# The degree count's matmuls with their operands swapped: the 49-wide one-hot stationary, the 128-wide one moving

## The reference, cut to what matters

```python
deg = jnp.maximum(jax.ops.segment_sum(jnp.ones(dst.shape, jnp.float32), dst, num_segments=6250), 1.0)
...
deg_isqrt = 1.0 / jnp.sqrt(node_deg)
f0 = f0 * deg_isqrt                      # features before the edges gather them
...
s_mid = s_mid * deg_isqrt                # sums of messages after the edges
```

## Time and profile before

| | |
|---|---|
| median of 3 timed runs | 4400.84 us (4399.68 to 4402.47) |
| profiled execution: span | 4400.9 us |
| PE busy / PEld busy in the span | 4086.7 us (93%) / 3374.9 us (77%) |
| DVE, ACT, POOL busy | 2987.8, 2610.6, 2599.1 us |
| node loop, 91.2 to 440.6 us: PE busy | 349.4 of 349.4 us |

### The profile page before, as it was taken

The page is one execution under the profiler, slowest core; times in us unless marked ns, Lnnn a source line. Parts: engine busy times, 40 slices in busy tenths (PEclk is TensorE's granted clock), DMA queues, the critical chain, the costliest instruction groups (busy, mean ns, idle before and its releaser), DMA issues. The chain is left out here.

```text
span 4400.9 us, 84837 instructions
## 1 busy us (share of the span) xinstructions
PE 4086.7 (93%) x19450; PEld 3374.9 (77%) x19450; DVE 2987.8 (68%) x5419; ACT 2610.6 (59%) x8831; POOL 2599.1 (59%) x2378
## 2 busy tenths in 40 slices
PE   4999599999999999999999999999985888888887
PEld 3888488888888888888888888888985777777776
DVE  5666699999999999999999999997666000000000
ACT  1444587888788878887888787776232222222222
POOL 3444577777777777777777777775113233333332
PEclk8999799999999999999999999999967999999999
DMA  3333333443444333433443444433223455555554
GB/s 117 103 101 98 116 103 103 104 104 103 104 104 104 104 104 104 103 103 104 104 104 103 103 103 104 104 103 85 79 80 107 147 153 152 155 161 156 152 161 119
DMA packets 432067, 497.39 MB, mean 113 GB/s; under 512 B 253111, under 2 KB 343707, under 8 KB 417707
## 3 DMA queue, kind: packets, MB, share of 16 engines
q0 software_dynamic: 105984, 260.17, 22.1%
q1 hardware_dynamic: 326059, 236.92, 18.8%
HBM read 433.72 MB, written 63.07 MB: 113 GB/s over the span
## 5 line engine op out<-in xcount | busy, mean ns | idle before, releaser
L615 POOL DMA_INDIRECT k_x<-gather_table,edges_src x1760 | 1995.9, 1134 | 576.9 <-issue 446.4
L632 ACT ACTIVATE k_x<-k_x,edges_y 128x64 f32<-128x64 f32 x5280 | 1303.0, 335 | 4.9 <-DMA k_x<-gather_table,edges_src 4.9
L738 PE MATMUL edges_ps_sum<-k_x,edges_hot_y 128*128 128x256 f32 x3520 | 1094.2, 393 | 0.5 <-issue 0.5
L738 PE MATMUL edges_ps_sum<-k_x,edges_hot 128*128 128x256 f32 x3520 | 1048.1, 379 | 0.0
L639 ACT ACTIVATE edges_hot_y<-edges_hot,edges_y 128x128 f32<-128x128 f32 x1760 | 562.4, 390 | 506.9 <-DVE edges_hot L678 506.9
L727 PE MATMUL edges_ps_edge<-k_w_e,edges_hT 100*128 100x256 f32 x3520 | 836.4, 380 | 7.8 <-ACT edges_hT L625 7.8
L694 DVE TENSOR_TENSOR k_x<-k_x,edges_ps_edge 128x768 f32<-128x768 f32 x880 | 794.4, 941 | 0.0
L738 PEld LDWEIGHTS edges_ps_sum<-k_x,edges_hot_y 128*128 128x128 f32 x3520 | 633.6, 190 | 175.3 <-issue 107.1
L727 PEld LDWEIGHTS edges_ps_edge<-k_w_e,edges_hT 100*128 100x128 f32 x3520 | 670.8, 191 | 101.5 <-issue 7.6
L738 PEld LDWEIGHTS edges_ps_sum<-k_x,edges_hot 128*128 128x128 f32 x3520 | 670.0, 190 | 91.1
L1341 DVE TENSOR_TENSOR experts_raw<-experts_ps_y,experts_b 128x256 f32<-128x256 f32 x112 | 42.3, 419 | 908.7 <-PE experts_ps_y L1297 908.7
(11 more groups left out here) (233 smaller groups left out, 3996.6 us busy)
## 6 DMA issues: line engine op xcount, KB each, us to landing
experts_w<-in_w SPq DMA_DIRECT2D x112, 1024.0 KB
k_x<-gather_table,edges_src POOLq DMA_INDIRECT x1760
edges_el<-el_hi SPq DMA_DIRECT2D x880, 20.0 KB
edges_el<-el_lo SPq DMA_DIRECT2D x440, 20.0 KB
nodes_el<-in_el SPq DMA_DIRECT2D x46, 170.0 KB, 2.4
el_hi<-nodes_el_hi SPq DMA_DIRECT2D x46, 170.0 KB, 1.9
el_lo<-nodes_el_lo SPq DMA_DIRECT2D x46, 170.0 KB, 2.0
experts_b<-in_b SPq DMA_DIRECT2D x56, 128.0 KB
```

The source lines that it names most:

```text
L615: nc.gpsimd.indirect_dma_start(out=rows[k][:, j, :], out_offset=None, in_=K.table_d.rearrange("t p d -> (t p) d"), in_offset=bass.Indirect ...
L632: x = nc.scalar.activation(Z[k % 2][:, j, MUL * (i + 1):MUL * (i + 2)], rows[k][:, j, 0:MUL], ACT.Identity, scale=y[k][:, j, 1 + i:2 + i])
L738: x = t.matmul(into[:, :, o, :], rows_hot[k % 2][:, j, :], msg[k % 2][:, j, o * D:(o + 1) * D], start=j == 0 and o == 0, stop=j == GC - 1, ...
```

## The change

The stationary and the moving operand of `count` trade places, so the sum comes out transposed: 49 partitions × 128 columns. It takes 128 columns of the bank `sums` in place of 49. None of the count's matmuls starts an accumulation now; one f32 matmul of zeros at the head of PE's list starts the whole used part of the bank (386 columns). At the end DVE copies the 49 × 128 degrees to SBUF (`deg_rows`), PE transposes them into `ps_T[0]`, and DVE clamps from there.

```diff
-        ps_c, deg = sums[:, 0:2 * (P + 1)], sums[:, 2 * (P + 1):2 * (P + 1) + NT]
+        ps_c, deg_T = sums[:, 0:2 * (P + 1)], sums[0:NB, 2 * (P + 1):2 * (P + 1) + P]
+        deg_rows = m.sb("deg_rows", [NB, P])
...
             for n in range(NEL, NT):
                 hots(n, n % 2)
+            dve.wait_ge(c["counted"], NT)
             dve.wait_ge(c["context"], NT)
-            v.tensor_scalar(K.dis[:, :], deg, 1.0, None, ALU.max).then_inc(c["clamped"], 1)
+            v.tensor_copy(deg_rows[:, :], deg_T).then_inc(c["deg_rows"], 1)
+            dve.wait_ge(c["deg"], 1)
+            v.tensor_scalar(K.dis[:, :], ps_T[0][:, 0:NT], 1.0, None, ALU.max).then_inc(c["clamped"], 1)
             dve.wait_ge(c["dis"], 1)
...
             def count(n, k):
                 pe.wait_ge(c["hot"], n + 1)
-                first, last = (isinstance(n, int) and n == e for e in (0, NT - 1))
+                last = isinstance(n, int) and n == NT - 1
                 for j in range(UC):
-                    z = t.matmul(deg, hot_lo[k][:, :, j], hot_hi[k][:, :, j], start=first and j == 0,
+                    z = t.matmul(deg_T, hot_hi[k][:, :, j], hot_lo[k][:, :, j], start=False,
                                  stop=last and j == UC - 1, skip_group_check=True)
                 z.then_inc(c["counted"], 1)
...
+            t.matmul(sums[:, 0:2 * (P + 1) + P], K.zeros[:, 0:P], K.zeros[:, 0:2 * (P + 1) + P], start=True, stop=False,
+                     skip_group_check=True)
             turn(0, 0)
...
             context(NT - 1, (NT - 1) % 2)
+            pe.wait_ge(c["deg_rows"], 1)
+            t.transpose(ps_T[0][:, 0:NB], deg_rows[:, :], K.ident[0:NB, 0:NB]).then_inc(c["deg"], 1)
```

More of the change, by code:

```diff
@@ L302, in nodes @@
             "shift", "var", "iota", "xn", "turned", "xnT", "fm", "kv", "queries", "fm_used", "k_parts", "q_parts",
-            "exps", "v", "k", "q", "res", "context", "f_scaled", "f_out", "built", "el_hi", "el_lo")}
+            "exps", "v", "k", "q", "res", "context", "deg_rows", "deg", "f_scaled", "f_out", "built", "el_hi", "el_lo")}
         el_in, el_out = ([m.sem(f"{z}{k}") for k in range(2)] for z in ("el_in", "el_out"))
```

## The result

The changed kernel takes 4691.79 us, the median of three runs (4691.65 to 4693.98), against 4400.84 us before: a ratio of 1.0662, with a 95% interval of 1.0643 to 1.0681. It is 291 us slower. The forecast was 4381 us, with a range of 4308 to 4490. The profiled execution has a span of 4692.2 us.

The account below looks back on a forecast made before the run. The prediction took PE's own instruction list to bound the node loop. It summed 4400.9 - 0 (pairs) - 20.3 (clock) + 0.8 (end) = 4381.4 us, with a range of 4308 to 4490.

Parts of the forecast that it names:

- What bounds the loop: Node loop: PE's own list sets the step, 7.28 us; DVE has 4.8 us of work in a step and stays covered.
- The pairs: Count's 1568 load and matmul pairs in the node loop: stay at 99.4 ns, 0 us; bounds 57 ns and 260 ns.
- rival B: Count's pairs: moving columns are the slow side, up to 260 ns a pair, 4653 us in full, 4487 halfway; chance 0.27.
- A: Count's pairs: matmul takes its columns at the array's pace, 57 ns a pair, 4315 us; chance 0.24.
- The clock: Node loop: a count 2.6 times as dense ends the clock drops behind it, -20.3 us; at worst 0.
- The end and the head: Stage's end: new copy, transpose and hand-overs, +0.8 us (0.6 to 1.2); zeros matmul at the head covered, 0.
- C: Node loop: pairs stay at 99 ns and the clock drops stay too, 4401.7 us, no change; chance 0.06.
- D: Count's pairs: moving side slightly dearer, 107 to 111 ns, +12 to +18 us, drops gone, 4393 to 4399; chance 0.06.

Follow-up runs that it names:

- b_both: The kernel before with both operands of the count contiguous (other degrees counted): 4313.73 us, against a median of 4402.58 for the kernel before.
- b_mov: The kernel before with only the count's 49 moving columns contiguous (other degrees counted): 4325.28 us, against 4404.3 for the kernel before.
- b_sta: The kernel before with only the count's 128 stationary columns contiguous (other degrees counted): 4364.05 us, 40 less than the kernel before.
- run 4692: Not a separate experiment: the changed kernel itself, count's operands swapped against the kernel before, 4691.79 us against 4400.84, ratio 1.0662; its profiled span is 4692.2 us.
- a_step4: The changed kernel with stationary columns contiguous and moving ones 8 bytes apart (other degrees counted): 5087.41 us on a slower chip, kernel before 5006.76.
- b_split: The kernel before with its count in two groups of 16 matmuls, same result: 5069.11 us against 5097.16 on that chip, ratio 0.9955.
- a_both: The changed kernel with both operands of the count contiguous (other degrees counted): 4332.39 us, against a median of 4402.58 for the kernel before.
- a_mov: The changed kernel with only its 128 moving columns contiguous (other degrees counted): 4379.43 us, 312 less than the changed kernel.
- quad: The kernel before with both one-hots laid out 4 edges side by side, columns 8 bytes apart: 5007.92 us against 5097.16 on that chip, ratio 0.9825.
- a_split: The changed kernel with its count in four groups of 8 between the projection's products: 5247.54 us on a slower chip, 241 above the kernel before.

## Why the prediction was wrong

**What bounds the loop.** Right. PE's own list set the step, and every nanosecond of the pair came through 1568 times; the rest of the kernel kept its length. Only what was said of a shorter step did not hold: DVE's work in a step is not fixed at 4.8 us. In b_both it is 5.8 (busy 99% of a step of 5.9), hot_lo's compare taking 2.8 us in place of 2.3, and DVE is the bound there.

**The pairs: the step that failed, by its size.** The prediction bounded the new pair at 57 and 260 ns and took 99.4, on the ground that reading such columns might cost the same on either side, the wider of the two setting the pair. It measured 224 ns in the changed kernel: +196 us where 0 was put down. The failed assumption is that of equal cost. The 128-wide load does not pay 0.78 ns a column; it is over in 62.5 ns or less (b_mov), 0.49 ns a column. The 99 ns were those of the 49 moving columns at 1.67 ns each and 4 on top (b_sta), plus 13 that stay unexplained. So the wider operand was on the cheap side, and the swap moved it to the dear one. One sentence of the prediction had it nearly whole, in rival B: the 49 columns "fetched one by one from 64 bytes apart at up to 2.03 ns, clock or no clock". B's full case gave 4653 us, and the run 4692, with a cheaper pair (224 ns for B's 260) and a clock that B took to be unchanged. It had 0.27, and its farther half was left out of the range.

**What spoke for B and was passed over.** The pair's indifference to the clock was read rightly as a limit outside the array, and then B was given hardly more weight (0.27) than A (0.24), which needs the array's pace. The argument set against B, that f32 pairs are bound by their load, was of contiguous operands and says nothing of strided ones.

**The clock: the second step that failed, by its sign.** Expected was -20.3 us, since the count would be "2.6 times as dense". A pair held up by its fetch is no denser: 128 columns in 224 ns are 0.57 a nanosecond, 49 in 99 are 0.49. What changed is how long such a run lasts, 7.2 us in place of 3.2, and the clock fell in every step. The rest of a step takes 6.52 us in place of the 4.28 which a_step4 shows for the same list at a clock of 1.00: 2.24 us in each of 46 steps, some 103 us, where 20 were lost before. These 83 us, and 46 times the 0.18 us that a_step4 has above the 4.10 of the kernel before, 8 us, are the 91 us. The part that was right is that the 20 us hang on the count: b_split gets 17.5 of them with nothing but two shorter runs.

**The end and the head.** +0.8 us was put down, 0.8 was found (0.82 from context to clamp, against 0.04). The transpose takes one f32 pair of 0.34 us, not two. The rows of L512 were misread there, and with them the rule that an x2 of f32 is one call: its 0.40 us are the two transposes of a tile, with one pair each (98 pairs for 49 tiles). The matmul of zeros is hidden.

**Rivals.** A is what a_both shows: 55 to 59 ns and 4332 us, but only when both operands are contiguous, so its condition was not in the change. (The sum had 4315; the step is 6.19 us, not 5.9, and 0.2 of the difference is what the 49-wide loads cost the rest of a step.) C and D did not occur. E, a rival that I did not write down, is that the swap also loses the fast 128-wide load; a_mov shows it as the 85 ns at which the pair would have stood even with a cheap moving side.

## What to carry to other kernels

Before an operand's width is moved from one side of a matmul to the other, ask how each side is read: for bf16 here, strided moving columns cost about 1.67 ns for every 16 bytes opened, and a 128-wide load of columns 64 bytes apart takes 62.5 ns where a 49-wide one takes 85. The layout in SBUF is the lever here more than the order of the operands; interleaving only 4 edges in place of 32 (quad) left the writer its fast form and halved the pair. And a pair time that doesn't change with TensorE's clock (96 ns at 0.50, 99 at 1.00) was here the sign that operands are being waited for. Long runs of such pairs also cost the clock of what came behind them, and cutting the run in two gave that back in b_split (17.5 us); cut in four, the longer run of the changed kernel gave back 30 us only.

## What the runs showed of the hardware

- A moving bf16 operand of 128 columns takes 112 ns at 8 bytes, 220 at 16, and 210 to 214 at 64 (loads' spacing): 1.64 to 1.75 ns for each new 16 bytes. Neighbouring columns take 55 ns and columns 4 bytes apart 56: there no price of the lines shows.
- A 49-wide bf16 load at 64 bytes takes 85 ns, which fits the same price, while a 128-wide one at 64 bytes takes at most 62.5 ns, at 8 bytes at most 51, and a contiguous one 26 ns together with its matmul of 49 columns.
- With the 128-wide load strided too, the pair of 49 moving columns was 13 ns longer than with the moving side alone strided (99 against 86). With a 49-wide load and 128 moving columns it was 4 ns (loads' spacing 214 against 210). The cause stays open.
- Runs of fetch-bound pairs and the granted clock: no drop behind 2.75 us of them, a drop in 12 of 46 steps behind 3.18 us, in every step behind 7.0 to 7.3 us. These pairs stream 49 columns in 86 to 99 ns or 128 in 220 to 230. A run of 3.8 us of pairs with 128 columns in 119 ns (a_step4) brought none.
- Going from f32 pairs to 49-wide bf16 pairs and back costs 0.3 to 0.4 us of PE (a_split, a_step4). With 128-wide bf16 pairs one more such turn left the step at 7.3 us (b_split).
- DVE's bf16 compare of 128 x 1568 elements took 2.31 us with its value repeated along the inner dimension and 1.50 with runs of 4 values, both in loops in which POOL was busy for 98 to 99% of the time.
